# A transformer kernel's second attention: 32 rows of TensorE and a PSUM bank for each of four heads

## What is computed

```python
b, n, d = encodings.shape                      # 16 heads of 8 features
qkv = encodings @ attn_W + attn_b
qkv = qkv.reshape(b, n, H, 3 * HS).transpose(0, 2, 1, 3)
q, k, v = jnp.split(qkv, 3, axis=-1)
scores = jnp.einsum('bhki,bhqi->bhkq', k, q) / math.sqrt(HS)
mask = jnp.arange(n)[:, None] <= jnp.arange(n)[None, :]
scores = jnp.where(mask, scores, jnp.float32(NEG_INF))
prob = jax.nn.softmax(scores, axis=2)
combined = jnp.einsum('bhkq,bhkl->bhql', prob, v)
```

## Time and profile before

| | |
|---|---|
| timed runs | 835.46, 836.0, 837.83 us, median 836.0 |
| the profiled execution | 834.34 us, its span 832.6 us |
| mean granted TensorE clock of it | 0.969 |
| busy: PE, PEld, DVE, ACT, POOL | 758.5, 688.9, 511.0, 420.8, 424.4 us |
| second attention, first to last scores | 325.8 to 598.0 us |
| transfers on the queue of SP and ACT | 67872 packets, 68.6 MB |

### The profile page before, as it was taken

How to read it: one execution, slowest core, us unless ns; L and a number is a source line. 1 busy time by engine, 2 the same in 40 slices (tenths; PEclk the granted TensorE clock), 3 DMA queues, 4 the chain that set the end, 5 groups by cost and what they waited for, 6 DMA issues and landing times. The chain is left out here.

```text
span 832.6 us, 18673 instructions
## 1 busy us (share of the span) xinstructions
PE 758.5 (91%) x6472; PEld 688.9 (83%) x6472; DVE 511.0 (61%) x1678; ACT 420.8 (51%) x1019; POOL 424.4 (51%) x519
## 2 busy tenths in 40 slices
PE   5787699799999997999999999999989599999994
PEld 4677689799999996777778787787779599999994
DVE  4687764254444466768787888867656344444437
ACT  2455445244444432755766666665655144444455
POOL 3247777155555550423444565665576255555530
PEclk9899979899999999999999999999999799999998
DMA  7981111233433134232223332233011233334138
GB/s 261 315 351 50 48 48 55 71 101 94 121 100 103 56 90 133 89 118 81 77 82 103 115 121 81 78 91 107 20 38 44 66 88 102 94 98 126 55 93 231
DMA packets 78164, 87.42 MB, mean 105 GB/s; under 512 B 12744, under 2 KB 66602, under 8 KB 77944
## 3 DMA queue, kind: packets, MB, share of 16 engines
q1 hardware_dynamic: 67872, 68.60, 26.9%
q0 software_dynamic: 9216, 17.34, 6.3%
q10 hardware_dynamic: 984, 0.29, 0.2%
HBM read 48.59 MB, written 39.65 MB: 106 GB/s over the span
## 5 line engine op out<-in xcount | busy, mean ns | idle before, releaser
L1145 ACT ACTIVATE hT<-bank,bias_T 128x256 f32<-128x256 f32 x448 | 175.4, 475 | 213.3 <-PE bank L788 213.2
L520 POOL DMA_INDIRECT y_rows<-yo,row_cur x160 | 157.6, 985 | 147.2 <-DVE yo L1608 120.4
L1698 DVE TENSOR_REDUCE negp<-bank 128x2 f32<-128x512 f32 (+1 forms) x192 | 128.1, 686 | 55.5 <-PE bank L852 52.9
L809 PE MATMUL bank<-w_s,hT 128*128 128x128 f32 x1280 | 155.9, 275 | 0.0
L809 PEld LDWEIGHTS bank<-w_s,hT 128*128 128x128 f32 x1280 | 150.0, 192 | 0.0
L558 POOL TENSOR_SCALAR_AFFINE_SELECT pt<-pt 128x512 f32<-128x512 f32 x128 | 79.5, 643 | 136.5 <-ACT pt L1205 136.4
L505 POOL DMA_INDIRECT x_slots<-xr,slot_u x128 | 128.8, 1006 | 39.5 <-issue 33.4
L1205 ACT ACTIVATE pt<-bank 128x512 f32<-128x512 f32 x192 | 107.7, 596 | 75.2 <-PE bank L880 62.8
L788 PE MATMUL bank<-xT_hl,w_hl 128*128 128x256 f32 x960 | 136.3, 292 | 3.3 <-DVE w_hl L1581 2.6
L788 PEld LDWEIGHTS bank<-xT_hl,w_hl 128*128 128x128 f32 x960 | 121.5, 193 | 4.0 <-DVE w_hl L1581 3.0
L1608 DVE TENSOR_TENSOR yo<-bank,b_b 128x256 f32<-128x256 f32 x80 | 34.0, 424 | 146.5 <-PE bank L809 146.5
(11 more groups left out here) (199 smaller groups left out, 1237.6 us busy)
## 6 DMA issues: line engine op xcount, KB each, us to landing
xg<-x_slots SPq DMA_DIRECT2D x80, 136.0 KB, 2.2
w_s<-in_L_ffn_w SPq DMA_DIRECT2D x32, 256.0 KB, 3.2
qk_rows<-qks SPq DMA_DIRECT2D x16, 512.0 KB, 4.3
bdk<-qk_rows SPq DMA_DIRECT2D x192, 32.0 KB
qc<-qk_rows SPq DMA_DIRECT2D x48, 128.0 KB, 2.8
x_slots<-xg SPq DMA_DIRECT2D x1, 5440.0 KB, 21.2
y_rows<-xg SPq DMA_DIRECT2D x1, 4096.0 KB, 15.0
bdk<-y_rows SPq DMA_DIRECT2D x1, 4096.0 KB
```

Of the source, the lines that this page charges most:

```text
L520: pool.indirect_dma_start(y_rows, bass.IndirectOffsetOnAxis(ap=row_cur[:, g % ROWS, j:j + 1], axis=0), yo[:, g % RING, j, :], None, bounds ...
L809: m = pe.matmul(yb(w, l)[:, j * P:(j + 1) * P], hT[:, w % 2, f, j * P:(j + 1) * P], wt[:, f, :], start=(f == 0), stop=(f == FT - 1))
L1145: a = act.activation(hT[:, w % 2, f, :], HB[2 * (w % 2) + f // 2][:, (f % 2) * 256:(f % 2) * 256 + 256], ACT.Silu, bias=bias_T[:, b0 + f:b ...
L1698: dve.tensor_reduce(dst, AB[(g + k) % 2][:, :].rearrange("p (j k) -> p j k", j=heads), AX.X, ALU.max, negate=True).then_inc(S.amax_done, 1)
```

## The change

Keys and queries lie in `kh` and `qh`, 32 rows for each of four heads: 24 rows with the three parts of 8, then one row of ones in the keys, and the negated maxima in the queries. Each head has its own PSUM bank (0 to 3, `front_banks`), in which 384 numbers a row are used: 128 and 256. `scores` replaces `pass1` and `pass2`: one call makes first scores of two heads of the unit one ahead and second scores of two heads of the unit two behind, in 8 matmuls of 24 or 25 rows, then two masks. It is called twice a step, k = 0 and 1, and the two pairs of banks change places. `max_b` reduces two banks with two instructions, one over 128 and one over 256. The maxima are transposed once and copied to `negs`, from where SP brings them to the queries' rows by two transfers per unit (`neg_rows`, semaphores `neg_in`). `restack` becomes `split_heads`, with 24 transfers of 8 rows; `kh` and `qh` hold three sequences instead of two. An exponential reads 384 numbers of two banks, and there are two a unit instead of three; GpSimd's two selects each wait for one of them. The zeroing of `bdk` and its rows of ones are gone; GpSimd sets all of `kh` to ones before the stage. In `attn_b_end` the same calls are made for the last two units, and `out_project(t, 0)` is moved ahead of `first_mm(1, 0)`.

```diff
+PARTS = 3
+QK_LOADS = 2 * PARTS * GRP
+UNITS = GRP * SEQS
...
-        bank = [ctx.enter_context(nc.psum_tensor(f"bank{k}", [P, 512], F32)) for k in range(8)]
+        front_banks = ctx.enter_context(nc.psum_tensor("front_banks", [P, 4, 512], F32))
+        bank = [front_banks[:, k, :] for k in range(4)] + [ctx.enter_context(nc.psum_tensor(f"bank{k}", [P, 512], F32)) for k in range(4, 8)]
...
-        bdk = sb("bdk", [P, 2, GRP, 4, SEQ], F32R)
+        kh = sb("kh", [P, 3, GRP, SEQ], F32R); qh = sb("qh", [P, 3, GRP, SEQ], F32R)
+        v_ext = sb("v_ext", [P, 2, 2, HEADS, 32])
...
-        pt = sb("pt", [P, 2, 3, 512])
-        qc = sb("qc", [P, 2, GRP, SEQ], F32R)
+        pt = sb("pt", [P, 2, 2, 3, 2, P])
...
-        v_ext = sb("v_ext", [P, 2, 2, HEADS, 32])
-        negp = sb("negp", [P, 2, 2, P])
+        negp = sb("negp", [P, 2, P]); negs = sb("negs", [P, 2, P], F32R)
...
-            def restack(t, par):
+            def split_heads(t, par):
                 n = 2 * t + par
-                rows_stored, k_in, q_in = ((S.qks_stored0, S.bdk_in0, S.qc_in0), (S.qks_stored1, S.bdk_in1, S.qc_in1))[par]
                 sp.wait_ge(S.hilo_done, n + 1)
-                need(sp, k_in, 16 * 12 * t)
-                need(sp, q_in, 48 * t)
-                sp.dma_start(qk_rows[par], qks[:, par, :, :, :].bitcast(F32)).then_inc(rows_stored, 16)
-                sp.wait_ge(rows_stored, 16 * t + 16)
-                need(sp, S.c_done, 3 * GRP * (n - 1))
+                need(sp, qk_in[(n - 2) % 3], 16 * QK_LOADS * ((n - 2) // 3 + 1))
+                sp.dma_start(qk_rows[par], qks[:, par, :, :, :].bitcast(F32)).then_inc(qks_stored[par], 16)
+                sp.wait_ge(qks_stored[par], 16 * t + 16)
+                need(sp, S.c_done, 2 * GRP * (n - 2))
                 rows = qk_rows[par].rearrange("(g r) a b t -> r g a b t", g=GRP)
-
-                for part, half in enumerate((0, 1, 0)):
-                    for j in range(4):
-                        r = HD * j
-                        sp.dma_start(bdk[32 * part + r:32 * part + r + HD, par, :, j, :].bitcast(F32), rows[r:r + HD, :, half, 1, :]
-                                     ).then_inc(k_in, 16)
-                for part, half in enumerate((0, 0, 1)):
-                    sp.dma_start(qc[32 * part:32 * part + 32, par, :, :].bitcast(F32), rows[:, :, half, 0, :]).then_inc(q_in, 16)
+                for dst, which, halves in ((kh, 1, (0, 1, 0)), (qh, 0, (0, 0, 1))):
+                    for part, half in enumerate(halves):
+                        for j in range(4):
+                            r = 32 * j + HD * part
+                            sp.dma_start(dst[r:r + HD, n % 3, :, :].bitcast(F32), rows[HD * j:HD * j + HD, :, half, which, :]
+                                         ).then_inc(qk_in[n % 3], 16)
+            def neg_rows(t, par, g):
+                n, U = 2 * t + par, 2 * GRP * t + GRP * par + g
+                sp.wait_ge(S.neg_set, U + 1)
+                need(sp, S.c_done, 2 * (U - 3))
+                for c in range(2):
+                    sp.dma_start(qh[8 * PARTS:P:32, n % 3, g, c * P:c * P + P].bitcast(F32), negs[c:P:32, g % 2, :].bitcast(F32)).then_inc(neg_in[U % 4], 16)
             def attn_b_pair(i):
                 for h in range(2):
-                    if valid(i + 3):
-                        y_load(i + 3, h)
-                    if valid(i + 1):
-                        restack(i + 1, h)
+                    for g in range(GRP):
+                        if valid(i):
+                            neg_rows(i, h, g)
+                        if g == 1 and valid(i + 3):
+                            y_load(i + 3, h)
+                        if g == 2 and valid(i + 1):
+                            split_heads(i + 1, h)
...
             sp.wait_ge(S.rows_zeroed, 16)
-            sp.dma_start(bdk[:, :, :, :, :].bitcast(F32).rearrange("p a g j t -> p (a g j t)"), y_rows.rearrange("(p r) d -> p (r d)", p=P)
-                         ).then_inc(S.bdk_zeroed, 16)
-            sp.wait_ge(S.bdk_zeroed, 16)
-
-            sp.wait_ge(S.const_pool, N_CONST_POOL)
-            for par in range(2):
-                for j in range(4):
-                    r = 96 + HD * j
-                    sp.dma_start(bdk[r:r + 1, par, :, j, :].bitcast(F32), oT[0:1, :, :]).then_inc(S.bdk_ones, 16)
...
                 pool.wait_ge(S.row_set, g + 1)
                 if c == 0:
                     if l == 0:
-
-                        pool.wait_ge(S.bdk_zeroed, 16)
+                        pool.wait_ge(S.rows_zeroed, 16)
...
-                pool.memset(negp[:, :, :, :], 0.0)
+                pool.memset(kh[:, :, :, :].bitcast(F32), 1.0)
+                pool.memset(negp[:, :, :], 0.0)
...
             def causal(t, par, g):
                 U = 2 * GRP * t + GRP * par + g
-                pool.wait_ge(S.exp_done, 3 * U + 3)
-                first = pt[:, g % 2, 0:2, :].rearrange("p u (j q) -> p (u j) q", j=2)[:, :, 0:P]
-                second = pt[:, g % 2, 2, :].rearrange("p (j q) -> p j q", j=4)
-                for blk in (first, second):
-                    a = pool.affine_select(out=blk, in_=blk, compare_op=ALU.is_ge, fill=0.0, base=0,
-                                           pattern=[[0, 4], [1, P]], channel_multiplier=-1)
-                a.then_inc(S.aff_done, 1)
+                for k in range(2):
+                    pool.wait_ge(S.exp_done, 2 * U + k + 1)
+                    blk = pt[:, g % 2, 1 - k, 0:2, :, :].rearrange("p c j q -> p (c j) q")
+                    pool.affine_select(out=blk, in_=blk, compare_op=ALU.is_ge, fill=0.0, base=0,
+                                       pattern=[[0, 4], [1, P]], channel_multiplier=-1).then_inc(S.aff_done, 1)
             def add_ob(i):
...
-            def pass1(t, par, g, k):
...
+            OB, MB, XB, ZB = bank[4:8]
+            def scores(t1, p1, g1, t2, p2, g2, k):
+                U1, U2 = 2 * GRP * t1 + GRP * p1 + g1, 2 * GRP * t2 + GRP * p2 + g2
+                n1, n2 = 2 * t1 + p1, 2 * t2 + p2
...
+            def scores(t1, p1, g1, t2, p2, g2, k):
+                U1, U2 = 2 * GRP * t1 + GRP * p1 + g1, 2 * GRP * t2 + GRP * p2 + g2
+                n1, n2 = 2 * t1 + p1, 2 * t2 + p2
+                first, second = (2 * k, 2 * k + 1), (2 - 2 * k, 3 - 2 * k)
+                if valid(t1):
+                    if g1 == 0 and k == 0:
+                        pe.wait_ge(qk_in[n1 % 3], 16 * QK_LOADS * (n1 // 3 + 1))
+                    need(pe, S.amax_done, 2 * (U1 - 1) + k + 1)
+                    need(pe, S.exp_done, 2 * (U1 - 3) + k)
+                if valid(t2):
+                    if k == 0:
+                        pe.wait_ge(neg_in[U2 % 4], 32 * (U2 // 4 + 1))
+                    pe.wait_ge(S.amax_done, min(2 * (U2 + 3) + k, 2 * UNITS))
+                    need(pe, S.exp_done, 2 * (U2 - 1) + k + 1)
+                for wide in (True, False):
+                    if valid(t1):
+                        for j in first:
+                            q = qh[32 * j:32 * j + 8 * PARTS, n1 % 3, g1, :]
+                            keys = kh[32 * j:32 * j + 8 * PARTS, n1 % 3, g1, :]
+                            if wide:
+                                pe.matmul(bank[j][:, P:3 * P], q[:, P:SEQ], keys, start=True, stop=False)
+                            else:
+                                pe.matmul(bank[j][:, 0:P], q[:, 0:P], keys[:, 0:P], start=False, stop=False)
+                    if valid(t2):
+                        for j in second:
+                            q = qh[32 * j:32 * j + 8 * PARTS + 1, n2 % 3, g2, :]
+                            keys = kh[32 * j:32 * j + 8 * PARTS + 1, n2 % 3, g2, :]
+                            if wide:
+                                m = pe.matmul(bank[j][:, P:3 * P], keys[:, 0:P], q, start=True, stop=True)
+                            else:
+                                m = pe.matmul(bank[j][:, 0:P], keys[:, P:SEQ], q[:, P:SEQ], start=True, stop=True)
+                if valid(t2):
+                    m.then_inc(S.c_done, 1)
+                if valid(t1):
+                    for j in first:
+                        m = pe.matmul(bank[j][:, 0:3 * P].rearrange("p (c k) -> p c k", c=3)[:, 0:3:2, :], ident_r[:, :],
+                                      cmask[:, :].unsqueeze(1).broadcast_to([P, 2, P]), start=False, stop=True)
+                    m.then_inc(S.a_done, 1)
             def neg_transpose(t, par, g):
                 U = 2 * GRP * t + GRP * par + g
-                pe.wait_ge(S.amax_done, 3 * U + 3)
+                pe.wait_ge(S.amax_done, 2 * U + 2)
                 need(pe, S.neg_set, U)
-                for qt in range(2):
-                    m = pe.transpose(MB[:, qt * P:qt * P + P], negp[:, g % 2, qt, :], ident[:, :])
-                m.then_inc(S.negT_done, 1)
-
-            def pass2(t, par, g, k):
...
-                        g1, g2, g3 = (shifted_group(i, h, g, -k) for k in (1, 2, 3))
```

(51 more changed lines are left out.)

83 lines of the change are left out of this document (17 added, 66 removed).

## The result

The changed kernel takes 1006.5 us (median of 4 runs, 1000.68 to 1011.01) against 835.7 for the kernel before in the same comparison: a ratio of 1.2036, 95% interval 1.1962 to 1.2109. That is +171 us where +135 was forecast. The profiled execution took 1009.12 us, with a span of 1007.4 us and a mean granted clock of 0.853.

What follows compares the result with a forecast made beforehand. TensorE's instruction order bounds the second attention; after the change SP's queue would, at 26.4 us a sequence against 17.3. Terms +127.4, +5.0 and +2.9 make +135.3 us, so 971 us, range 912 to 1035.

Steps and rivals of the forecast that it cites:

- rivals 3 and 4: Tiles bring no overlap, starts 0.12 us apart: 991 us, chance 0.16; and crowded transfers, slower issues and landings: 1027, chance 0.07.
- rival 2: Row groups run side by side, not slower: 822 us, chance 0.05; sign: masks within 0.4 us of the first score.
- The turn: Once-a-sequence loop through SP's queue and TensorE: 14.4 + 11.0 us, plus 1.0 for clock, 26.4 us.
- the maxima's 2.84: SP's two transfers of group 3's maxima: second issued 0.34 us later, landing at about 2.5.
- The piece on TensorE: From TensorE's restart in step 1 to the next split's end: 11.0 us, plus 1.0 for lowered clock.
- The tiles' distance: Between starts of the eight 32-row score matmuls on TensorE: 0.085 us taken, 0.68 for eight.
- The half step: Each `scores` call waits for readers of its banks, a closed loop; two make a step of 4.95 us against 4.32.
- Half 1: Second half step: scores and masks, handover, VectorE's pair of maxima (1.11), way back; 2.43 us.
- Half 0: First half step, through the maxima's transpose, ScalarE's copy (0.27) and exponential (0.82); 2.52 us.
- The start: First sequence's loads, 24 issues instead of 15, on the path: +2.9 us; GpSimd's memset at nothing.
- The sum: Whole kernel: +127.4 for 14 sequences, +5.0 for the other two, +2.9 at the start; +135.3 us.
- Rival 1: SP's loop is hidden and only the half steps count: 879 us, chance 0.08.

Runs made afterwards that it cites:

- e1: Changed kernel with the 24 loads split: 12 key loads behind group 3's maxima, 12 query loads behind group 0's of the next sequence; 916.3 us, ratio 1.0996.
- e3: Changed kernel with the maxima's transfers issued from ScalarE's queue behind its exponentials instead of SP's; 910.3 us, ratio 1.0901.
- e4: Changed kernel in which SP waits for the 24 loads to land before issuing group 3's maxima; 1032.1 us in one execution.
- e12: Changed kernel with the two inner loops of the 24 loads exchanged (rows 0, 8, 16, then 32); 1016.8 us in one execution, kernel before 884.6.
- e9: Changed kernel with GpSimd's memset of kh moved to the constants at the program's start; 1053.4 us beside 884.6, ratio 1.1893.
- e10: e1 plus filler matmuls, their results unread, at two places of each step (some steps have none); 892.0 us, ratio 1.0663.
- e13: e10 plus the exchanged load order and the early memset of kh; 937.7 us beside 884.5, ratio 1.0602.

## Why the prediction was right, and where its terms were off

Right: the bottleneck moved to SP's queue, by the mechanism that was forecast. TensorE idles once a sequence, released by `qh`<-`negs`; 24 issues stand ahead of group 3's two; taking the maxima out from behind them removes the waits (e1, e3). The size was met less well. The measured 1006.5 lies just above the forecast's own neighbourhood (922 to 1005), in the part up to 1035 that was added for rivals 3 and 4, and neither of them came true: the first scores are not 0.12 us apart, issues took 0.342 us and not 0.417, and the store landed in 2.63 us and not in 5.2. That a slow landing of the loads, which was not in the sum, fell into this allowance is luck. Two of the signs missed as well: a turn is 28.29 us where 25 to 27 was named, and the masks come 0.38 us after the first score, which was named as the sign of rival 2. (The 0.9 us named there as the sign of being right doesn't fit the sum, which has 0.77.)

- **The turn**, forecast 26.4, measured 28.29. In the turn shown its SP chain is 16.3 us for 14.4. The store landed in 2.63 us (3.3 taken), the 24 issues took 8.3 (8.2). **The mis-sized term is the maxima's 2.84**: 5.33 measured. By themselves they take 2.31, two issues of 0.5 included (e4). The other 3.0 us are the loads ahead of them, which were taken to land as fast as they are issued but lagged by 4.95 (e4). With the loads reordered the term is 2.30 (e12), and 2.84 would have been enough. I had looked at the number of issues and not at which rows follow each other. The store gave back 0.7 of the 2.5 us that the term lacked.
- **The piece on TensorE**, forecast 11.0 + 1.0 for the clock, measured 11.8, but by two errors. Two halves at the lower clock, the second with the projection in it, took 3.00 and 3.50 us (510.64, 513.64, 517.14), 1.8 over the 4.7 that two take at full clock; 1.0 was taken. At full clock the piece would be 11.8 - 1.8 = 10.0, where 11.0 was forecast.
- **The tiles' distance.** 0.085 us was the middle of 0.049 and 0.12. Even its lower end is above what the rows show:

```profile
517.14 0.18 PEld L863 LDWEIGHTS front_banks<-kh,qh 24*128 24x128 f32 x2
517.14 0.18 PEld L871 LDWEIGHTS front_banks<-qh,kh 25*128 25x128 f32 x2
517.24 0.19 PEld L865 LDWEIGHTS front_banks<-kh,qh 24*128 24x128 f32 x2
517.25 0.19 PEld L873 LDWEIGHTS front_banks<-qh,kh 25*128 25x128 f32 x2
```

  Four weight loads of 0.18 us start together, the next four 0.1 later, and the mask follows at 517.52: eight in 0.38 us, 0.047 each, with the change of rows in it. Rival 3 (no overlap) is refuted, and so is the forecast's reading that the rule of the Trainium skill ("TensorE: Matmul & The Clock Gate", LDWEIGHTS) puts the eight loads one behind the other. The Trainium skill ("TensorEngine Tiling (Array Packing)", Key Properties) says that different tiles can load weights and multiply in parallel, and the trace agrees: four loads of 0.18 us start within 0.01 us.
- **The half step.** Half 1, forecast 2.43, measured 2.19. VectorE's pair is 0.43 and 0.68 us, with starts 0.34 apart, so 1.02 for 1.11; the way back to TensorE is 0.25 instead of 0.05. Half 0, forecast 2.52, measured 2.27 (517.14 to 519.41). The 2.53 of the next one is near the forecast by luck, since the router's `sel` held up its transpose. ScalarE's operations were right, 0.28 (0.27) and 0.81 (0.82), but mostly it isn't the last: of 39 waits at the end of a half 0 VectorE ends 30. A step at full clock is 4.5 to 4.7 us for 4.95.
- **The start**, forecast +2.9, measured +9.3. The first store is issued at 318.42 us (before 315.06), which fits two casts of 3.25 and 3.61 us (before 1.33 and 1.30) beside GpSimd's copy and memset; I had put the memset at nothing, with 3 us if its cover were gone. The rest is the slow landing of the first 24 loads: the wait is 9.2 us here, 9.5 in e9 and 5.2 in e12.
- **The sum.** In the profiled executions the difference is +174.8, 39.5 us over the forecast (in the medians 36). 13 turns at + 1.9 are 25 us, the start another 6.4 (9.3 less 2.9), the end of the program 3.6: 35 us. The other 4.8 lie in the stage outside these turns and are not assigned.
- **Rival 1** (SP hidden, 879) is what e1, e3, e10 and e13 built. Its step of 4.95 is near what e10 (5.03) and e13 (4.97) show at a clock of 0.93, and 892 and 1.0602 x 836 = 886 stand near 879. The agreement is partly luck: the step of halves alone is shorter (4.5 to 4.7), and projections, fillers and the clock add what the forecast had in the halves. But e1 at 916 shows what it left out: with short waits all along and no filler the clock is 0.77, and that costs 24 us or more.
- **Rival 2** (faster, 822) asked for eight scores under 0.25 us. They take 0.38, nearer to it than to the forecast. It failed at VectorE's 1.02 and the handovers, as was held against it, at the maxima that came late, and at the clock.

What stays open: how much of the 161.9 us is clock in the changed kernel itself (0.75 between 360 and 760 us), since fillers were tried on e1's order alone; what makes the 6% by which e10 and e13 still lie behind the kernel before, for which the closed loop is argued and not shown; and by what mechanism the order of the rows makes the loads slow.

## What to carry to other kernels

A short urgent transfer costs what stands ahead of it in its queue twice: the issues (24 x 0.342 us here) and then their landing (up to 4.95 us after the last). Look for what is queued behind a block of issues, and move the block or the urgent one (-90 us here) before counting engine time. When many narrow loads are needed, try an order in which consecutive ones write neighbouring rows and not rows 32 apart (1.2036 to 1.1445 here). And an order in which TensorE often waits for the reader of a bank pays in clock too, although no single wait is long (0.77 in e1).
